# Cross-attention and a mixture-of-experts block on one core: the prologue reordered, with contiguous loads, slots filled by DMA, and keys projected ahead of the layer norm

## The reference

```python
x = x + xattn(layernorm(x), ctx, ctx)      # 16 heads of 16 channels, softmax over 1024 keys
x = x + ffn(layernorm(x))
# xattn: q = Q@W_Q.T+b_Q, k = K@W_K.T+b_K, v = V@W_V.T+b_V
#        softmax(q k^T / 4) v, then @W_O.T+b_O
# ffn:   (silu(x@sw1) * (x@sw3)) @ sw2
#        + for 8 experts gelu(x@ew1[e]) @ ew2[e], weighted by the gates of the best 2
#        (sigmoid router plus bias)
```

## Time and profile before

| | us |
|---|---|
| median of 3 runs | 384.77 |
| the runs | 383.74, 384.77, 386.97 |
| profiled execution, its own time | 386.84 |
| its span, first to last instruction | 385.0 |
| PE busy | 365.8 (95%) |
| DVE busy | 300.1 (78%) |
| ACT busy | 211.4 (55%) |
| POOL busy | 126.2 (33%) |
| DMA queue, its packets' share of 16 engines | 28.3% |
| mean granted clock of PE | 0.978 |

### The profile page before, as it was taken

How to read it: one execution, slowest core, us unless ns; L and a number is a source line. 1 busy time by engine, 2 the same in 40 slices (tenths; PEclk the granted TensorE clock), 3 DMA queues, 4 the chain that set the end, 5 groups by cost and what they waited for, 6 DMA issues and landing times.

```text
span 385.0 us, 7131 instructions
## 1 busy us (share of the span) xinstructions
PE 365.8 (95%) x2732; PEld 228.0 (59%) x2732; DVE 300.1 (78%) x459; ACT 211.4 (55%) x375; POOL 126.2 (33%) x170
## 2 busy tenths in 40 slices
PE   5958999999999999999999999999999799999996
PEld 2756575333333333333733453489899688999985
DVE  6896978799999999999499317076699966787875
ACT  5637533698999899989478857621122231412211
POOL 5040553103043333323233222000277574016800
PEclk9999999699999999999999969999999999999999
DMA  7965880016060514234100200020032213003301
GB/s 240 376 224 204 267 316 5 2 40 189 5 224 4 186 43 143 86 106 125 60 3 3 60 3 3 2 57 2 2 109 85 82 59 107 0 3 93 127 0 54
DMA packets 23465, 35.56 MB, mean 92 GB/s; under 512 B 5620, under 2 KB 17268, under 8 KB 21876
## 3 DMA queue, kind: packets, MB, share of 16 engines
q1 hardware_dynamic: 23432, 35.12, 28.3%
HBM read 27.15 MB, written 7.34 MB: 90 GB/s over the span
## 4 chain that ended last, share of the span: by engine, by line
PE 79%; DVE 12%; issue 3%; ACT 3%; POOL 1%; POOLq 0%; ACTq 0%; DVEq 0%
PE psum L1059 38%; PE psum L1205 17%; PE psum L1129 13%; PE psum L1136 7%; DVE negm L956 5%; PE psum L1147 2%; DVE x_sb L942 2%; ACT PB L716 1%; DVE nt L823 1%; PE psum L1218 1%; DVE KS L924 1%; ACT TMP L761 1%; DVE xn L827 1%; PE psum L1188 1%; PE psum L1071 1%
## 5 line engine op out<-in xcount | busy, mean ns | idle before, releaser
L956 DVE TENSOR_REDUCE negm<-psum 128x1 f32<-128x1024 f32 x128 | 154.1, 1223 | 12.2 <-PE psum L1136 11.6
L716 ACT ACTIVATE PB<-psum 128x512 f32<-128x512 f32 x256 | 138.0, 599 | 34.6 <-PE psum L1129 26.8
L1129 PE MATMUL psum<-QS,KS 64*128 64x512 f32 x256 | 93.3, 466 | 1.1 <-DVE rows L858 0.6
L1136 PE MATMUL psum<-KS,QS 64*128 64x512 f32 x276 | 89.1, 454 | 1.9 <-DVE negm L956 1.6
L1205 PE MATMUL psum<-PB,VA 128*17 128x256 f32 x1024 | 82.3, 396 | 2.1 <-ACT TMP L761 2.1
L731 ACT ACTIVATE PB<-psum 128x512 f32<-128x512 f32 x40 | 22.1, 597 | 98.6 <-PE psum L1059 98.6
L1129 PEld LDWEIGHTS psum<-QS,KS 64*128 64x128 f32 x256 | 38.6, 189 | 52.3 <-ACT PB L716 40.5
L628 POOL TENSOR_SCALAR R<-RAW 128x512 fp32r<-128x512 f32 x32 | 21.5, 670 | 99.7 <-PE psum L1059 75.7
L1059 PE MATMUL psum<-XT,R 128*128 128x512 f32 x192 | 46.7, 392 | 0.0
L1205 PEld LDWEIGHTS psum<-PB,VA 128*17 128x17 f32 x1024 | 17.5, 96 | 46.7 <-issue 35.7
L631 POOL TENSOR_TENSOR R<-RAW,R 128x512 fp32r<-128x512 f32 x32 | 43.2, 1349 | 2.7
(11 more groups left out here) (139 smaller groups left out, 373.4 us busy)
## 6 DMA issues: line engine op xcount, KB each, us to landing
RAW<-in_ew_dram SPq DMA_DIRECT2D x32, 256.0 KB, 2.7
KS<-ks_d SPq DMA_DIRECT2D x24, 256.0 KB
QS<-qs_d SPq DMA_DIRECT2D x48, 128.0 KB
ks_d<-SWH SPq DMA_DIRECT2D x8, 512.0 KB, 4.0
qs_d<-SWH SPq DMA_DIRECT2D x4, 512.0 KB, 5.0
RAW<-in_sw_dram SPq DMA_DIRECT2D x6, 256.0 KB, 2.7
x_sb<-in_x_dram SPq DMA_DIRECT2D x2, 512.0 KB, 6.0
PB<-in_ctxT_dram SPq DMA_DIRECT2D x2, 512.0 KB, 7.2
```

The costliest lines, as they stand in the source:

```text
L716: act.activation(PB[:, n % PR, i * N:(i + 1) * N], bank[t % 3], ACT.Exp, scale=DK ** -0.5).then_inc(exp_done, 1)
L956: dve.tensor_reduce(negm[:, g % 2, r // QT, r % QT:r % QT + 1], psum[:, k0:k0 + 2, :].rearrange("p a n -> p (a n)"), AX.X, ALU.max, negate ...
L1129: pe.matmul(bank[t % 3], KS[s][rows, j, kp * P:(kp + 1) * P], QS[s][rows, j, :], start=True, stop=True).then_inc(scores_done, 1)
L1136: return pe.matmul(ring_bank(("max", m), half), QS[s][rows, j, qt * P:(qt + 1) * P], KS[s][rows, j, :], start=True, stop=True)
```

## The change

- Loads: the context and the weights are laid out beforehand so that each partition reads one contiguous run; x (and the output) is taken as 4 consecutive tokens to a partition. The key weights and the first context piece are loaded first, then x; the output weights and the bias rows are loaded later, behind the first stack.
- Order of work: the K projections of context half 0, for both halves of the heads, come before the transposes of x. Two of the four V jobs, and the transposes of batch 1, move behind the first maximum. All other jobs are spread over the 22 first maxima by the table `beside_max`; the second computation of the later maxima goes.
- Slots: the memsets of slots 1 and 2 and ACT's filling of their keys go; instead SP copies the fourth rows of slot 0 into them (two transfers of 32 rows of 8 KB for each slot).
- QS is loaded by three transfers instead of six, each of 32 rows of 8 KB; the source names the 16 rows of `qs_d` twice, `broadcast_to([2, DK, GH * N])`, the two copies being the outer count. This holds for all eight stacks.
- `load_bias(0)` also waits until stacks 1 and 2 have landed.
- The lo parts of the second batch's context move from DVE to POOL; the splits of router and output weights move behind the first maxima's on POOL.
- The job "B" goes; the value bias is added to each group's output instead, on POOL (groups 0 to 5) by one instruction more, on DVE (groups 6 and 7) in the instructions that are there.

```diff
-    jobs = [("T", 0, 0, 0), ("T", 0, 1, 0)]
-    for m in range(2):
-        jobs += [("K", 0, m, 0), ("K", 0, m, 1), ("Q", 0, m, 0)]
+    jobs = [("K", 0, 0, 0), ("K", 0, 1, 0), ("T", 0, 0, 0), ("T", 0, 1, 0), ("K", 0, 0, 1), ("Q", 0, 0, 0)]
+    jobs += [("K", 0, 1, 1), ("Q", 0, 1, 0)]
     jobs += [("V", 0, i, 0) for i in range(4)] + [("T", 1, 0, 0), ("T", 1, 1, 0)]
-    FIRST_KQ1 = len(jobs)
     for m in range(2):
         jobs += [("K", 1, m, 0), ("K", 1, m, 1), ("Q", 1, m, 0)]
-    jobs += [("V", 1, i, 0) for i in range(4)] + [("B", 0, 0, 0)]
+    jobs += [("V", 1, i, 0) for i in range(4)]
...
-    steps = [("stats", 0), ("rstd", 0), ("split", 0), ("norm1", 0), ("split", 1), ("split", 2), ("split", 3)]
-    steps += [("job", 0), ("job", 1), ("job", 2), ("mid", 0), ("mid", 1), ("job", 3), ("mid", 2), ("job", 4)]
-    steps += [("mid", 3), ("mid", 4), ("split", 4), ("stats", 1), ("rstd", 1), ("job", 5), ("mid", 5)]
-    steps += [("norm1", 1), ("job", 6), ("mid", 6), ("job", 7), ("mid", 7), ("split", 5), ("split", 6)]
-    for n in range(8, FIRST_KQ1):
-        steps.append(("job", n))
-        if n == 9:
-            steps += [("zero", 1), ("zero", 2)]
-    steps += [("keys", 1), ("keys", 2), ("mid", FIRST_KQ1 - 2), ("mid", FIRST_KQ1 - 1)]
-    n = FIRST_KQ1
+    steps = [("split", 0), ("split", 1), ("stats", 0), ("rstd", 0), ("split", 2), ("norm1", 0), ("split", 3)]
+    steps += [("job", 0), ("mid", 0), ("job", 1), ("job", 2), ("job", 3), ("mid", 2), ("mid", 3), ("mid", 1)]
+    steps += [("job", 4), ("mid", 4), ("job", 5), ("mid", 5), ("split", 4), ("job", 6), ("mid", 6)]
+    steps += [("stats", 1), ("rstd", 1), ("job", 7), ("mid", 7), ("norm1", 1), ("job", 8), ("job", 9)]
+    beside_max = {0: [10], 2: [11], 3: [12, 13], 5: [14], 7: [15], 9: [16], 11: [17], 13: [18], 14: [19],
+                  16: [20], 17: [21], 19: [22], 21: [23]}
     for m in range(LEAD):
         steps.append(("max", m))
-        if m % 2 and n < NJ:
-            steps.append(("job", n))
-            n += 1
-        if m == UG - 3:
-            steps.append(("wo",))
+        steps += [("job", n) for n in beside_max.get(m, [])]
+        if m == 2:
+            steps += [("split", 5), ("split", 6)]
+        if m == 4:
+            steps += [("mid", 12), ("mid", 13)]
         if m == UG + 1:
             steps.append(("negmax", 0))
-    steps += [("job", i) for i in range(n, NJ)] + [("mid", NJ - 1), ("clear",)]
+    steps.append(("clear",))
...
+        def stack_count(g):
+
+            return 16 * (2 * TERMS * (g // SLOTS + 1) + 2 * (g // SLOTS) + (2 if g % SLOTS else 0))
...
-            cT = ctxT.rearrange("(k p) t -> p k t", p=P)
-            xt = x.rearrange("(t p) d -> p t d", p=P)
-            sp.dma_start(x_sb[:, 0:4, :], xt[:, 0:4, :]).then_inc(ld_x[0], 16)
-            sp.dma_start(wraw[:, WK], wkT.rearrange("(k p) n -> p k n", p=P)).then_inc(ld_w[WK], 16)
-            for tb in range(2):
-                sp.dma_start(craw[:, :, tb * N:(tb + 1) * N], cT[:, :, tb * N:(tb + 1) * N]).then_inc(ld_ctx[tb], 16)
-            sp.dma_start(wraw[:, WQ], wqT.rearrange("(k p) n -> p k n", p=P)).then_inc(ld_w[WQ], 16)
+            xt = x.rearrange("(b p t) d -> p b t d", b=B, p=P)
+            sp.dma_start(wraw[:, WK], wkT).then_inc(ld_w[WK], 16)
+            sp.dma_start(PB[:, 0, :], ctxT[0]).then_inc(ld_ctx[0], 16)
+            sp.dma_start(x_sb[:, 0:4, :], xt[:, 0]).then_inc(ld_x[0], 16)
             sp.dma_start(small[:, :], smalls).then_inc(ld_small, 16)
-            sp.dma_start(x_sb[:, 4:8, :], xt[:, 4:8, :]).then_inc(ld_x[1], 16)
-            sp.dma_start(wraw[:, WV], wvT.rearrange("(k p) n -> p k n", p=P)).then_inc(ld_w[WV], 16)
-            sp.dma_start(craw[:, :, T:], cT[:, :, T:]).then_inc(ld_ctx[2], 16)
-            sp.dma_start(woraw, woP).then_inc(ld_wo, 16)
-            sp.dma_start(rows[:, :], bias_rows.rearrange("(a n) -> a n", a=1).broadcast_to([P, D + NE]))\
-              .then_inc(ld_rows, 16)
-
+            sp.dma_start(PB[:, 1, :], ctxT[1]).then_inc(ld_ctx[1], 16)
+            sp.dma_start(wraw[:, WQ], wqT).then_inc(ld_w[WQ], 16)
+            sp.dma_start(wraw[:, WV], wvT).then_inc(ld_w[WV], 16)
+            sp.dma_start(x_sb[:, 4:8, :], xt[:, 1]).then_inc(ld_x[1], 16)
+            sp.dma_start(PB[:, 2:4, :], ctxT[2:4].rearrange("c p n -> p c n")).then_inc(ld_ctx[2], 16)
...
-                    sp.wait_ge(ks_init, g + 1)
-                    sp.wait_ge(qs_init[g], 1)
+                    sp.wait_ge(ks_init, 1)
+                    sp.wait_ge(qs_init, 1)
+                    if g:
+
+                        for stk in (KS, QS):
+                            sp.dma_start(raw(stk[s][BIAS_ROW::RSTEP, :, :]), raw(stk[0][BIAS_ROW::RSTEP, :, :]))\
+                                .then_inc(stk_loaded[s], 16)
...
                 for c, term in enumerate((0, 1, 0)):
-                    for tb in range(2):
-                        sp.dma_start(raw(QS[s][tb * HP + c:(tb + 1) * HP:RSTEP, :, :]), qs_d[b, m, term, :, l])\
-                            .then_inc(stk_loaded[s], 16)
+
+                    src = qs_d[b, m, term, :, l].rearrange("(o d) j t -> o d (j t)", o=1).broadcast_to([2, DK, GH * N])
+                    sp.dma_start(raw(QS[s][c::RSTEP, :, :]), src).then_inc(stk_loaded[s], 16)
 
             def load_bias(g):
                 if g:
                     sp.wait_ge(exp_done, tile_at[("negmax", g)] + 1)
                 else:
                     sp.wait_ge(*freed(("negmax", g)))
+                    for s in range(1, SLOTS):
+                        sp.wait_ge(stk_loaded[s], stack_count(s))
...
-                if c == 2:
+                if c == 3:
                     load_stack(0)
+                    sp.dma_start(woraw, woP).then_inc(ld_wo, 16)
+                    sp.dma_start(rows[:, :], bias_rows.rearrange("(a n) -> a n", a=1).broadcast_to([P, D + NE]))\
+                        .then_inc(ld_rows, 16)
...
-                elif st[0] == "zero":
-                    pool.memset(raw(QS[st[1]][:, :, :]), 0.0).then_inc(qs_init[st[1]], 1)
-                elif st[0] == "wo":
-
-                    pool.wait_ge(ld_small, 16)
-                    pool.tensor_scalar(rw[:, 0], rw_raw, 1.0, 1.0, ALU.mult, ALU.mult).then_inc(pool_chain, 1)
-                    pool.wait_ge(ld_wo, 16)
-                    pool.tensor_scalar(wo_hl[0], woraw, 1.0, 1.0, ALU.mult, ALU.mult).then_inc(pool_chain, 1)
-                    pool.wait_ge(pool_chain, 2)
-                    pool.tensor_tensor(rw[:, 1], rw_raw, raw(rw[:, 0]), ALU.subtract).then_inc(pool_split, 1)
-                    pool.tensor_tensor(wo_hl[1], woraw, raw(wo_hl[0]), ALU.subtract).then_inc(pool_split, 1)
-
-            splits_done = [2]
+                elif st[0] == "split" and splits[st[1]][:2] == ("c", 1):
+
+                    if st[1] == 5:
+                        pool.wait_ge(xn_ready, 8)
+                    pool.wait_ge(split_hi, st[1] + 1)
+                    c = 2 + splits[st[1]][2]
+                    pool.tensor_tensor(R1[:, 4 + c, :], PB[:, c, :], raw(R1[:, c, :]), ALU.subtract)\
+                        .then_inc(ctx_lo[1], 1)
+
+            splits_done = [1]
...
+            pool.wait_ge(ld_small, 16)
+            pool.tensor_scalar(rw[:, 0], rw_raw, 1.0, 1.0, ALU.mult, ALU.mult).then_inc(pool_chain, 1)
+            pool.wait_ge(pool_chain, 1)
+            pool.tensor_tensor(rw[:, 1], rw_raw, raw(rw[:, 0]), ALU.subtract).then_inc(rw_split, 1)
             negated_maxima(0)
+            pool.wait_ge(ld_wo, 16)
+            pool.tensor_scalar(wo_hl[0], woraw, 1.0, 1.0, ALU.mult, ALU.mult).then_inc(pool_chain, 1)
+            splits_done[0] += 1
+            pool.wait_ge(pool_chain, splits_done[0])
+            pool.tensor_tensor(wo_hl[1], woraw, raw(wo_hl[0]), ALU.subtract).then_inc(pool_split, 1)
             pool.wait_ge(xn_ready, 8)
-            b_job = jobs.index(("B", 0, 0, 0))
-            pool.wait_ge(job_free[b_job % 4], b_job // 4 + 1)
+            pool.wait_ge(ld_rows, 16)
...
-                    pool.tensor_tensor(RC, U[g % 2], RC, ALU.mult).then_inc(rc_ready, 1)
+                    pool.tensor_tensor(RC, U[g % 2], RC, ALU.mult).then_inc(rc_scaled, 1)
+                    pool.wait_ge(rc_scaled, g - 1)
+                    hg = (g - 2) % HG
+                    pool.tensor_scalar(RC, RC, bv_sb[:, hg:hg + 1], None, ALU.add).then_inc(rc_ready, 1)
...
-                if kind == "B":
-                    dve.wait_ge(jobs_done, n + 1)
-                    dve.wait_ge(ld_rows, 16)
-                    dve.tensor_tensor(bo_sb[:, :], bank[n % 4][:, 0:D], bo_sb[:, :], ALU.add)\
-                       .then_inc(job_free[n % 4], 1)
...
-                    for _ in range(1 if m < UG - 4 else 2):
-
-                        maxima(m, 1)
-                        last = maxima(m, 0)
-                    last.then_inc(ring_full, 1)
+                    maxima(m, 1)
+                    maxima(m, 0).then_inc(ring_full, 1)
```

(53 more changed lines are left out.)

30 lines of the change are left out of this document (16 added, 14 removed).

## The result

The changed kernel takes 469.94 us in the median of 4 runs (464.78 to 472.42) against 384.63 for the kernel before: a ratio of 1.2159 (95% interval 1.2052 to 1.2266). The profiled execution took 464.78, with a span of 463.0, 78.0 more than the 385.0 of before.

A forecast was written before the change was run, and what follows sets the result against it. The prediction took PE (79% of the span) as the bound. To the profiled 386.84 us it added 29.7 in the prologue and 49.0 in the steady phase, 465.5, less 2.07: 463 us, range 440 to 490.

The forecast's parts named there:

- Two engines for each QS load: All stack loads: source outer count 2 confines each transfer to two engines, 5.26 us a load, 15.8 a stack.
- First maxima at 41.2: Prologue: PE idles from 24.9 until stack 0's QS lands at 41.2; maxima begin 9 us later than at 32.27.
- 20.3 + 2.4: Prologue: store of queries issued at 20.3, plus 2.4 us to the KS issue, taken as 22.4.
- Unit 0 at 93.4, +29.7: End of prologue: bias rows queue behind stack 2 and six stores, so unit 0 starts at 93.4 against 63.72.
- stack 1 at maximum 16: Prologue: maximum 16 needs stack 1, so PE was to wait again until about 65.
- Waits of 8.2 in groups 1 to 5: Steady phase, unit 10: QS needed at 119.26 lands at 127.5 in group 2's row, so PE stands 8.2 us.
- Clock behind them, forecast 1.6 each: After each steady-phase wait: two units at the lower clock, 0.82 us more each, so 1.6 a group (bounds 0 and 3.2).
- Sum: 465.5: Whole kernel, profiled execution: 386.84 + 29.7 + 49.0 = 465.5 us.
- The 463 in the median: Whole kernel: 465.5 less the 2.07 by which the earlier profiled execution exceeded its median.
- Rival A: QS copies spread over all 16 engines; unit 0 comes 4.2 us earlier, 380.5 us in all; chance 0.11.
- DVE paces the stretch behind the first maxima: Prologue, in the 380.5 us case: DVE's 22 reductions keep this stretch at 31 us; job B's removal saves at most 0.4.
- Rival C: Sixteen engines, but thinner maxima let the clock fall; ten slower units take the 4.2 back, about 388 us; chance 0.03.

The follow-up runs named there:

- e2_rows_outermost: Changed kernel, with the QS source reordered so that the 16 rows are the outer count and the two copies the inner one: 387.96 us, ratio 1.0075.
- e8_rows_2_outermost: Changed kernel, with each QS load's source given outer count 2 of nonzero stride (two rows) and 16 copies inside: 467.55 us in one run.
- e1_six_loads: Changed kernel, with each stack's QS again loaded by six transfers of 16 rows: 386.2 us, ratio 1.003 to the kernel before.
- e6_all_free_jobs_ahead: Changed kernel with six QS loads, and V jobs, batch 1's transposes and lo parts, and second-batch context splits ahead of the first maximum: 383.7 us, ratio 0.9939.

## Why the prediction held, and where it did not

- **Two engines for each QS load: right, and shown.** Share 0.13 alone in the queue, at 27 GB/s an engine (I took 24.9); undone by the order of two counts (e2_rows_outermost), brought back without a stride of zero (e8_rows_2_outermost). The rule in the Trainium skill, page "DMA: Bandwidth & Descriptors", section "Why a DMA increments its semaphore by 16 and not by 1", agrees with counts of 2, 4, 8 and 16 here.
- **First maxima at 41.2: measured 42.46.** The wait began at 24.5, as forecast. The sum has a slip, 20.3 + 2.4 being 22.7 and not 22.4; and the 2.4 us from the store of queries to the issue of KS were 1.0 here (20.47 to 21.47).
- **Unit 0 at 93.4, +29.7: measured 90.69, +27.0.** The bias rows set it, behind three stacks, as the sum had it: SP waited 2.0 us for stack 2, until 82.4 (forecast 85.0), and the rows came 8.3 later (forecast 8.4). A step inside was wrong: PE did not wait for stack 1 at maximum 16. It came there at about 68, and the stack was in place.
- **Waits of 8.2 in groups 1 to 5: measured 7.61, 7.93, 9.19, 8.04 and 9.15, mean 8.4.**
- **Clock behind them, forecast 1.6 each: more, some 2.0.** From unit 0 to the end are 372.3 us; less the 321.3 of before and 41.9 of waits that leaves 9.1, 1.8 each. But the 321.3 have two stretches at the lower clock of their own, the one of the earlier trace rows and, in the kernel before,

```profile
226.00:231.00 5.00, 5.00 (x27) 2.50 (x27) 0.95 (x5) 2.29 (x5) 0.07 (x1) 0.50 0.01 2
```

where e1_six_loads has none,

```profile
63.00:130.00 67.00, 65.19 (x611) 25.52 (x613) 63.88 (x57) 58.60 (x110) 20.24 (x31) 1.00 0.24 76
190.00:250.00 60.00, 59.36 (x493) 27.70 (x492) 31.59 (x69) 42.86 (x80) 17.63 (x19) 1.00 0.07 20
```

and needs 315.9 us (381.8 less 65.89). Against that, 14.5 us are left. The changed kernel is at the lower clock for 3.8 us behind unit 0 and for 26.2 us in all behind the five waits. By the 0.82 us that a unit of 2.13 loses, the 26.2 cost 10, 2.0 for each wait (an estimate), and the 3.8 cost 1.5; some 3 us of the 14.5 stay unplaced.
- **Sum: 465.5 for a profiled execution, measured 464.78.** That it fits to 0.7 is in part luck: the prologue came 2.7 below the forecast, the steady phase 2.0 above (51.0 against 49.0). The 463 in the median was 7 us low. I took the 2.07 off that the profiled execution of before lay above its median; of the changed kernel the profiled one is the fastest run (clock 0.904), the others had 0.88 to 0.89. An execution with six long waits has six places at which the clock may stay low longer; that is how I read it, and no run tested it.
- **Rival A's working was wrong**, though nothing hung on it: with the loads spread the kernel would have been the same as before (1.003), not 4.2 us faster. I said that DVE paces the stretch behind the first maxima, 22 reductions in 31 us. PE does: its four added jobs are 4.5 us there. The maxima computed twice seem to have filled gaps only: with the four jobs ahead and no second maxima e6_all_free_jobs_ahead needs 30.8 us for the stretch, the kernel before 31.4 with them. Rival C, the clock taking the gain back, was nearer. At 28.5 I had the first maxima too early, too: 29.95 with three loads, 30.94 with six.
